# Third of four graph networks: where its last bias is added, how its last product is taken from the banks, and in which batches it is normalized

## The chip, the core and the metric

The kernel runs on one core of one Trainium2 chip. The metric is the device time of one execution in microseconds, as the median of several. The core has five engines with instruction streams of their own: TensorE (PE: matmuls and transposes, with weight loads shown as PEld), VectorE (DVE), ScalarE (ACT), GpSimd (POOL) and SyncE (SP, which here only issues DMAs). They synchronize through semaphores.

## The reference

1250 nodes with 768 features each, 20,000 edges. Four graph networks follow each other, and after each one the result is added to its input and normalized over the features. The third is this (its edge weights are normalized by the degrees, and every node also has an edge to itself):

```python
def _gcn(x, W, b, row, col, ew):
    x = x @ W
    deg = jax.ops.segment_sum(ew, col, num_segments=n) + 1.0
    dinv = jax.lax.rsqrt(deg)
    norm = dinv[row] * ew * dinv[col]
    agg = jax.ops.segment_sum(norm[:, None] * x[row], col, num_segments=n)
    return agg + (dinv * dinv)[:, None] * x + b
h = jax.nn.relu(x @ Wd + bd) @ Wu + bu + x          # 768 -> 24 -> 768
h = jax.nn.relu(_gcn(h, W1, b1, row, col, edge_weight))   # 768 -> 256
h = _gcn(h, W2, b2, row, col, edge_weight)                # 256 -> 768
x = _layernorm(x + h)                                # (v - mean) / sqrt(var + eps)
```

The fourth network starts with two products of every head with 64x64 matrices and then attends along the edges.

## The kernel before

The nodes are cut into NT = 10 tiles of P = 125 rows; `node_b` holds all tiles of the residual (125 x 10 x 768, f32), `node_a` is a buffer of the same size. Each engine has a program of its own. Between phases stands a barrier: `next_phase` (L478 to L482) drains the engine, adds to `phase_end` and waits until all five have done so.

**The phase of the graph sums.** SyncE issues seven loads behind the barrier (L1152 to L1156), the last of them `wadj`, 6250 KB of dense adjacency. TensorE transposes `node_b`, makes the bottleneck product (L1938, L1945), transposes again and makes the product with W1 (L1954). Then it sums over the graph with the dense adjacency, split into a high and a low part: two halves (c = 0 for the first layer, c = 1 for the second), in each ten tiles d, in each tile ten pieces t of three matmuls (L1968). Four banks are in turn, so tile q waits for the take of tile q - 4; the first tile of a half waits, piece by piece, for the low parts of the features (`feature_low`). VectorE takes each sum (`with_own`, two adds), applies the degrees, in the first half also the bias b1 and the relu (L2468, L2469), and makes the low part of the features of the tile before (`row_low_part(1, d - 1, agg1)`, L2447). Behind the first half's loop it makes the low part of tile 9, then the ten tiles of the second half follow.

**The last phase of the third network.** Behind the barrier SyncE issues the weights `gw2` (L1158, 768 KB), the last bias spread over 125 partitions (`gb2_row`, L1159, 375 KB), and eight small loads for the fourth network. TensorE transposes the aggregate (20 transposes), which ScalarE copies out, waits for ten loads on `bulk_loaded`, and makes ten tiles of the product with W2. Each tile has two halves of 384 columns in two banks; with four banks, tile n waits until tile n - 2 has been taken (`mm_taken`). One f32 matmul of the code is two instructions in the profile, so a tile is eight. VectorE does this for each tile, and then normalizes all ten:

```python
for g in range(2):
    v = slice(g * HD, (g + 1) * HD)
    chain.mark(dve.tensor_tensor(node_a[:, n, v], bank[...][0:P, 0:HD], gb2_row[:, v], op=ALU.add))      # L2482
chain.wait()
dve.tensor_tensor(node_b[:, n], node_b[:, n], node_a[:, n], op=ALU.add).then_inc(mm_taken, 1)            # L2484
dve.wait_ge(mm_taken, 2 * NT + n + 1)
dve_stats(dve, chain, node_b, n)                                                                       # L536
```

`dve_norm` is `dve_moments` over all tiles (one `bn_aggr` each, L542, and an add of eps for all, L545), the root of all on ScalarE (`act_sqrt`, L562), and `dve_scale`: a reciprocal (L551) and one scaling of 125x768 for each tile (L553). Then comes the next barrier. Behind it SyncE loads the mask of the fourth network (L1170), and TensorE transposes `node_b` (60 transposes) and makes the fourth network's transform (L1999, L2001).

`iota_row` (128 x 1254) holds the numbers 0, 1, 2, ... by which the second network picks its rows; nothing reads it after that network.

A `Chain` counts instructions of one engine on a semaphore: `mark` has an instruction signal it, `wait` waits for all that were marked.

## Time and profile before

| | us |
|---|---|
| runs | 3425.73, 3424.27, 3413.43; median 3424.27 |
| the profiled execution | 3441.28, of which the profile's span is 3439.5 |
| TensorE busy | 3240.6 |
| VectorE busy | 2173.2 |
| ScalarE busy | 1335.0 |
| GpSimd busy | 922.2 |
| mean granted clock of TensorE | 0.957 of full speed |

The profile is one execution, taken by the hardware profiler. Times in it are us from the span's start. The views used below: the *chain of waits* follows the work that ended last back from the end, each step to what released it; the *timeline* lists instructions in order of time, equal ones merged, with the idle time before them and what ended it in brackets; *stretches* give busy us of each engine with its number of instructions in a window, then the granted clock of TensorE (PEclk: 1.00 is 2.4 GHz, 0.50 is 1.2 GHz), the mean share of the 16 DMA engines that was busy, and what they moved. `arena` is the large buffer in which most tensors lie, `bank` a PSUM bank. SPq and DVEq stand for what an engine's queue did, issues and barriers.

### The profile page before, as it was taken

The page shows a single profiled execution, that of the slowest core. Times are in us where ns is not written, and L with a number is a line of the kernel's source. Part 1 is how long each engine was busy: PE and PEld are TensorE (multiplying, and loading weights), DVE is VectorE, ACT ScalarE, POOL GpSimd, SP SyncE. Part 2 cuts the span into 40 slices and gives each one's busy share as a digit, 9 for nine tenths or more (in the row PEclk, how much of TensorE's full clock was granted, in tenths as well). Part 3 has the DMA queues.
Part 4 walks back from the last instruction along what each step waited for, and adds up shares of the span by engine and source line. Part 5 has one row for each costly group of instructions (what it writes and reads, how often), then busy time and mean ns, then how long its engine had stood idle before and what let it go on. Part 6 is the DMA issues. An engine that isn't in the chain of part 4 may idle for free. (4 is left out here: it accounts for less than half of the span.)

```text
span 3439.5 us, 61775 instructions
## 1 busy us (share of the span) xinstructions
PE 3240.6 (94%) x20813; PEld 3025.1 (88%) x20813; DVE 2173.2 (63%) x4034; ACT 1335.0 (39%) x2527; POOL 922.2 (27%) x968
## 2 busy tenths in 40 slices
PE   6998989999998999999999999999989797899998
PEld 6886778888888999999988999999979495799998
DVE  7898456766777520137878401258868454499998
ACT  1344232333323111124446311134555211388885
POOL 1104534444554310014456200034456000000000
PEclk9999999999999999999999999999999797699997
DMA  3134353423213343347867533367767203000001
GB/s 81 46 105 139 97 137 83 101 50 100 61 31 92 109 142 100 102 157 242 242 207 235 171 111 101 101 203 242 238 204 228 92 1 76 12 1 0 0 0 46
DMA packets 164966, 386.06 MB, mean 112 GB/s; under 512 B 34418, under 2 KB 103583, under 8 KB 164758
## 3 DMA queue, kind: packets, MB, share of 16 engines
q0 software_dynamic: 47200, 173.39, 16.9%
q1 hardware_dynamic: 80074, 147.20, 15.2%
q10 hardware_dynamic: 37484, 62.75, 6.0%
q8 instruction: 124, 2.03, 0.2%
q14 instruction: 84, 0.69, 0.1%
HBM read 283.93 MB, written 99.32 MB: 111 GB/s over the span
## 5 line engine op out<-in xcount | busy, mean ns | idle before, releaser
L1877 PE MATMUL bank<-w_hi,xT_hi 128*125 128x384 f32 x1920 | 650.4, 339 | 0.0
L1878 PE MATMUL bank<-w_lo,xT_hi 128*125 128x384 f32 x1920 | 648.6, 338 | 0.0
L1879 PE MATMUL bank<-w_hi,xT_lo 128*125 128x384 f32 x1920 | 648.5, 338 | 0.0
L1563 ACT COPY arena<-bank 125x384 f32<-125x384 f32 x320 | 153.7, 480 | 793.2 <-PE bank L1879 762.5
L830 POOL DMA_INDIRECT arena<-y_early,edges x204 | 229.4, 1125 | 821.5 <-DMA y_late<-arena 320.4
L904 DVE SCALAR_TENSOR_TENSOR row_lo<-arena,edges,row_hi 128x768 fp32r<-128x768 f32 x300 | 304.2, 1014 | 124.4 <-ACT row_hi L873 84.1
L2345 DVE CAST w_hi<-w_raw 128x2304 fp32r<-128x2304 f32 x35 | 47.6, 1360 | 517.8 <-PE bank L1879 512.5
L1878 PEld LDWEIGHTS bank<-w_lo,xT_hi 128*125 128x125 f32 x1920 | 356.5, 186 | 0.1
L1877 PEld LDWEIGHTS bank<-w_hi,xT_hi 128*125 128x125 f32 x1920 | 356.5, 186 | 0.0
L1879 PEld LDWEIGHTS bank<-w_hi,xT_lo 128*125 128x125 f32 x1920 | 356.3, 186 | 0.1
L743 ACT ACTIVATE arena<-arena,low 125x1250 f32<-125x1250 f32 x170 | 227.7, 1339 | 327.7 <-DVE low L755 327.7
L780 PE MATMUL bank<-arena 125*125 (+1 forms) x2400 | 284.8, 276 | 0.0
L780 PEld LDWEIGHTS bank<-arena 125*125 125x125 f32 x2400 | 281.3, 195 | 0.0
L669 PE MATMUL bank<-h_hi,tsc 125*125 125x512 f32 x800 | 267.4, 408 | 1.3 <-DVE tsc L645 1.3
L1319 POOL DMA_INDIRECT order_d<-row_slot,place_slot x162 | 180.9, 1117 | 321.3 <-DMA order_d<-row_slot,place_slot 265.4
L755 DVE CUSTOM_DVE_ANT_0 arena<-arena 125x1250 f32<-125x1250 f32 x170 | 247.0, 1453 | 9.6 <-DVE arena L749 9.6
L763 PE MATMUL bank<-ident,arena 125*125 125x125 f32 x1700 | 225.9, 281 | 24.6 <-ACT arena L743 11.8
L763 PEld LDWEIGHTS bank<-ident,arena 125*125 125x125 f32 x1700 | 209.3, 195 | 27.7 <-ACT arena L743 17.9
L830 POOL DMA_INDIRECT arena<-y_late,idx_slot x168 | 193.9, 1154 | 126.2 <-issue 55.7
L1299 POOL DMA_INDIRECT w_slot<-inv_d,idx_slot x162 | 177.3, 1094 | 54.3 <-issue 51.5
L873 ACT ACTIVATE row_hi<-arena,edges 128x768 fp32r<-128x768 f32 x204 | 182.0, 932 | 24.6 <-PE bank L963 23.1
L669 PEld LDWEIGHTS bank<-h_hi,tsc 125*125 125x125 f32 x800 | 153.2, 192 | 39.6 <-DVE tsc L645 1.1
(359 smaller groups left out, 6685.7 us busy)
## 6 DMA issues: line engine op xcount, KB each, us to landing
y_early<-arena SPq DMA_DIRECT2D x200, 180.0 KB
w_raw<-in_L_gnn_W_dram ACTq DMA_DIRECT2D x30, 1152.0 KB, 6.4
arena<-own_mask_d SPq DMA_DIRECT2D x50, 585.9 KB
y_late<-arena SPq DMA_DIRECT2D x120, 180.0 KB
h_d<-arena ACTq DMA_DIRECT2D x40, 250.0 KB
arena<-in_L_gnn_W_dram SPq DMA_DIRECT2D x5, 1536.0 KB, 10.8
arena<-h_d ACTq DMA_DIRECT2D x30, 250.0 KB
wadj_d<-arena SPq DMA_DIRECT2D x10, 625.0 KB
```

What stands on the lines that cost most here:

```text
L669: ins = pe.matmul(bank[b][0:P, 0:w], x[:, u % 2, t], y, start=(t == 0 and i == 0), stop=(t == NT - 1 and i == 2))
L743: act.activation(sc, sc, ACT.Exp, scale=-1.0, bias=low[:, d % 4:d % 4 + 1], accum_out=den[:, d % 4:d % 4 + 1]).then_inc(weight_made, 1)
L755: dve.tensor_tensor_reduce(out=sc, in0=sc, in1=mask_row, scale=1.0, scalar=CEILING, op0=ALU.add, op1=ALU.min, accum_out=low[:, d % 4:d % 4 ...
L763: ins = pe.transpose(bank[c][0:P, t * P:(t + 1) * P], sc[:, (t0 + t) * P:(t0 + t + 1) * P], ident[0:P, 0:P])
L780: ins = pe.matmul(bank[b][0:P, 0:w], tsc[:, t], f, start=(t == 0), stop=(t == NT - 1))
L830: pool.indirect_dma_start(gathered[:, k], None, y, bass.IndirectOffsetOnAxis(ap=idx, axis=0)).then_inc(row_landed[k], 16)
L873: act.activation(hi_slot[k % HR], gathered[:, k], ACT.Copy, scale=order[:, p, W_AT:W_AT + 1]).then_inc(high_ready, 1)
L904: dve.scalar_tensor_tensor(lo, gathered[:, k], w, hi.bitcast(F32), op0=ALU.mult, op1=ALU.subtract).then_inc(tile_ready, 1)
L1319: pool.indirect_dma_start(order_d, bass.IndirectOffsetOnAxis(ap=place_slot[:, k:k + 1], axis=0), row_slot[:, k], None).then_inc(order_plac ...
L1877: pe.matmul(b, xT_hi[:, k, v], w_hi[:, h, k], start=(k == 0), stop=False)
L1878: pe.matmul(b, xT_hi[:, k, v], w_lo[:, h, k], start=False, stop=False)
L1879: ins = pe.matmul(b, xT_lo[:, k, v], w_hi[:, h, k], start=False, stop=(k == KD - 1))
```

## The change

The last bias of the third network, `gb2_row`, lies in `iota_row` instead of beside the weights, and is loaded one phase earlier, behind `wadj`, with a semaphore `gb2_loaded` of its own. VectorE adds it to the residual tiles during the first half of the graph sums: tile d behind the low part of tile d - 1, for d from 1 to 9, and tile 0 behind the low part of tile 9. The last product's banks are added straight to `node_b`, and the release of the banks is signalled by the second of these adds. The normalization is split: the moments of tiles 0 to 5 (`HEAD` = 6) come behind the statistics of tile 7, their scalings behind the statistics of tile 8, and the moments and scalings of the other four tiles at the end; ScalarE takes two roots in place of one. The waits on `bulk_loaded` go from ten loads to nine, and VectorE's is replaced by one on its own chain.

```diff
--- before.py
+++ after.py
@@ -381,7 +381,8 @@
         assert gcn_at <= w_at
         gw2 = cut(rest, KG2, D)
         zT = cut(rest + KG2 * D, KG2, N)
-        gb2_row = cut(rest + KG2 * D + KG2 * N, D, parts=P)
+        gb2_row = iota_row[0:P, 0:D]
+        HEAD = NT - 4
         wadj = cut(w_at, NT, NT, CT, parts=P)
         agg1 = cut(gcn_at, NT, G2, parts=P)
         assert gcn_at + NT * G2 <= w_at
@@ -428,6 +429,7 @@
         diag_made, s_spread, s_row_ready = sem("diag_made"), sem("s_spread"), sem("s_row_ready")
         w3_cleared, w3_loaded, w3_turned, w3T_ready = sem("w3_cleared"), sem("w3_loaded"), sem("w3_turned"), sem("w3T_ready")
         iota_ready, bias_loaded = sem("iota_ready"), sem("bias_loaded")
+        gb2_loaded = sem("gb2_loaded")
         far_marked, ln_taken, own_shifted, own_ready = sem("far_marked"), sem("ln_taken"), sem("own_shifted"), sem("own_ready")
         acc_cleared, ln_shifted, own_counted, ln_out = sem("acc_cleared"), sem("ln_shifted"), sem("own_counted"), sem("ln_out")
         mask_stored, mask_loaded = [sem(f"mask_stored{i}") for i in range(2)], sem("mask_loaded")
@@ -1154,9 +1156,9 @@
                          (gw1, a["L2_gnn_W1"].rearrange("(k p) c -> p k c", p=128)), (gb1_row, spread(a["L2_gnn_b1"], P))):
                 sp.dma_start(v, t).then_inc(bulk_loaded, 16)
             sp.dma_start(wadj.rearrange("p d s c -> p d (s c)"), wadj_d.rearrange("d p c -> p d c")).then_inc(wadj_loaded, 16)
+            sp.dma_start(gb2_row, spread(a["L2_gnn_b2"], P)).then_inc(gb2_loaded, 16)
             next_phase(sp)
             sp.dma_start(gw2, a["L2_gnn_W2"].rearrange("(k p) c -> p k c", p=128)).then_inc(bulk_loaded, 16)
-            sp.dma_start(gb2_row, spread(a["L2_gnn_b2"], P)).then_inc(bulk_loaded, 16)
             sp.wait_ge(w3_cleared, 2)
             for i, v in enumerate((a["L3_gnn_attn_l"], a["L3_gnn_attn_r"])):
                 for q in range(2):
@@ -1628,7 +1630,8 @@
                 act.copy(own_hi[1][:, d], agg1[:, d]).then_inc(feature_high, 1)
             next_phase(act)
             act_turn(act, "turn_act", zT, KG2)
-            act_sqrt(act, "sqrt_act", rstd[:])
+            act_sqrt(act, "sqrt_act", rstd[:, 0:HEAD])
+            act_sqrt(act, "sqrt_act", rstd[:, HEAD:NT])
             next_phase(act)
             act_turn(act, "turn_act", xT, KD)
             act.wait_ge(w3_turned, 1)
@@ -1970,7 +1973,7 @@
             next_phase(pe)
             pe_turn(pe, "turn_pe", agg2, KG2)
             pe.wait_ge(piece_taken, counts["turn_pe"])
-            pe.wait_ge(bulk_loaded, 16 * 10)
+            pe.wait_ge(bulk_loaded, 16 * 9)
             for n in range(NT):
                 if n >= 2:
                     pe.wait_ge(mm_taken, 2 * NT + n - 1)
@@ -2469,22 +2472,34 @@
                 dve.tensor_scalar(agg1[:, d], agg1[:, d], 0.0, dinv[:, d:d + 1], op0=ALU.max, op1=ALU.mult).then_inc(sum_taken, 1)
                 if d:
                     row_low_part(1, d - 1, agg1)
+                if d == 1:
+                    dve.wait_ge(gb2_loaded, 16)
+                if d:
+                    chain.mark(dve.tensor_tensor(node_b[:, d], node_b[:, d], gb2_row, op=ALU.add))
             row_low_part(1, NT - 1, agg1)
+            chain.mark(dve.tensor_tensor(node_b[:, 0], node_b[:, 0], gb2_row, op=ALU.add))
             for d in range(NT):
                 with_own(agg2[:, d], 1, d)
                 dve.tensor_scalar(agg2[:, d], agg2[:, d], dinv[:, d:d + 1], None, op0=ALU.mult).then_inc(sum_taken, 1)
             next_phase(dve)
-            dve.wait_ge(bulk_loaded, 16 * 10)
+            chain.wait()
             for n in range(NT):
                 dve.wait_ge(mm_made, 2 * NT + n + 1)
                 for g in range(2):
                     v = slice(g * HD, (g + 1) * HD)
-                    chain.mark(dve.tensor_tensor(node_a[:, n, v], bank[2 * (n % 2) + g][0:P, 0:HD], gb2_row[:, v], op=ALU.add))
+                    ins = dve.tensor_tensor(node_b[:, n, v], bank[2 * (n % 2) + g][0:P, 0:HD], node_b[:, n, v], op=ALU.add)
+                    if g == 0:
+                        chain.mark(ins)
+                ins.then_inc(mm_taken, 1)
                 chain.wait()
-                dve.tensor_tensor(node_b[:, n], node_b[:, n], node_a[:, n], op=ALU.add).then_inc(mm_taken, 1)
                 dve.wait_ge(mm_taken, 2 * NT + n + 1)
                 dve_stats(dve, chain, node_b, n)
-            dve_norm(dve, chain, node_b, node_b)
+                if n == HEAD + 1:
+                    dve_moments(dve, chain, range(HEAD))
+                if n == HEAD + 2:
+                    dve_scale(dve, chain, node_b, node_b, range(HEAD))
+            dve_moments(dve, chain, range(HEAD, NT))
+            dve_scale(dve, chain, node_b, node_b, range(HEAD, NT))
             next_phase(dve)
             for n in range(NT):
                 for g in range(3):
```

## Rows read from the trace of the kernel before

**Rows 1.** The page, busy time of the engines: us, share of the span, instructions.

```profile
PE 3240.6 (94%) x20813; PEld 3025.1 (88%) x20813; DVE 2173.2 (63%) x4034; ACT 1335.0 (39%) x2527; POOL 922.2 (27%) x968
```

**Rows 2.** The chain of waits, third network's last phase: start us, us, what ran.

```profile
2844.80 8.11 DMA arena<-in_L_gnn_b_dram
...
2853.05 4.80 PE bank L1979 x8
...
2857.97 1.03 DVE arena L2482 x2
...
2859.03 0.97 DVE arena L2484
2860.03 1.02 DVE stats L536 x2
...
2887.78 0.87 DVE moments L542 x10
```

**Rows 3.** The timeline of that phase: start us, us, engine, line, operation, count.

```profile
2844.39 2.35 PE L516 MATMUL bank<-ident,arena 125*128 125x125 f32 x20 [1.41 <-DVEq L481]
...
2889.37 5.99 DVE L553 TENSOR_SCALAR arena<-arena,moments,rstd 125x768 f32<-125x768 f32 x10
...
2895.44 1.95 SPq L1170 DMA_DIRECT2D arena<-mask_d  x2
```

**Rows 4.** Stretches of 1 us: busy us by engine, PEclk, DMA share, GB/s.

```profile
2845.00:2846.00 1.00, 1.00 (x12) 1.00 (x11) 0.00 (x0) 0.87 (x2) 0.00 (x0) 1.00 0.49 77
2846.00:2847.00 1.00, 0.75 (x7) 0.51 (x5) 0.00 (x0) 1.00 (x4) 0.00 (x0) 1.00 0.79 224
2847.00:2848.00 1.00, 0.00 (x0) 0.00 (x0) 0.00 (x0) 0.69 (x2) 0.00 (x0) 1.00 1.04 369
2848.00:2849.00 1.00, 0.00 (x0) 0.00 (x0) 0.00 (x0) 0.00 (x0) 0.00 (x0) 1.00 0.81 171
...
2850.00:2851.00 1.00, 0.00 (x0) 0.00 (x0) 0.00 (x0) 0.00 (x0) 0.00 (x0) 0.60 0.51 127
...
2857.00:2858.00 1.00, 1.00 (x5) 0.58 (x4) 0.03 (x1) 0.00 (x0) 0.00 (x0) 0.98 0.00 0
```

**Rows 5.** Who waited for whom; the bottleneck product in the chain, its clock.

```profile
PEld bank L1979 <- DVE arena L2484: 5.3, 8, 0.7
...
2712.76 20.21 PE bank L1945 x32
...
2720.00:2722.00 2.00, 2.00 (x5) 0.94 (x3) 1.77 (x3) 0.00 (x0) 0.00 (x0) 0.50 0.33 136
```

**Rows 6.** Graph sums: TensorE in the chain; VectorE's timeline where the halves meet.

```profile
2772.02 70.97 PE bank L1968 x600
...
2807.46 0.42 DVE L2463 TENSOR_TENSOR arena<-bank,own_hi 125x256 f32<-125x256 f32 x1 [1.43 <-PE bank L1968]
...
2809.17 0.98 DVE L2447 TENSOR_TENSOR own_lo<-arena,own_hi 125x256 fp32r<-125x256 f32 x2
...
2811.03 0.42 DVE L2463 TENSOR_TENSOR arena<-bank,own_hi 125x256 f32<-125x256 f32 x1 [0.88 <-PE bank L1968]
```

**Rows 7.** VectorE's timeline, normalization of the network before in seven and three tiles.

```profile
2671.52 4.22 DVE L553 TENSOR_SCALAR arena<-arena,moments,rstd 125x768 f32<-125x768 f32 x7
...
2677.75 0.35 DVE L542 BATCH_NORM_AGGREGATE moments<-stats 125x2 f32<-125x12 f32 x3
```

**Rows 8.** A stretch of 2 us after the adjacency load, and its first use.

```profile
2740.00:2742.00 2.00, 2.00 (x16) 2.00 (x15) 0.00 (x0) 1.41 (x4) 0.00 (x0) 0.75 0.00 0
...
2745.49 5.99 ACT L1620 CAST adj_hi<-arena 125x1280 fp32r<-125x1280 f32 x5
```

**Rows 9.** Stretches where the clock fell, and the fourth network's transform.

```profile
2690.00:2692.00 2.00, 0.09 (x1) 0.00 (x0) 0.00 (x0) 1.25 (x4) 0.00 (x0) 1.00 0.26 101
2692.00:2694.00 2.00, 1.95 (x4) 0.50 (x5) 0.00 (x0) 0.00 (x0) 0.00 (x0) 0.80 0.31 131
...
2909.00:2976.00 67.00, 67.00 (x213) 57.29 (x212) 11.11 (x27) 9.68 (x26) 0.00 (x0) 0.50 0.30 57
```

## The prediction

> **What bounds the kernel now.** I read the page first, then the chain of waits, then the stretch of the third network engine by engine. The page says that TensorE is busy for 94% of a span of 3439.5 us [rows 1], so a change on VectorE can only pay where TensorE waits. Apart from one load and ten adds in the phase before it, this change acts in the third network's last phase, between the barrier at 2844.4 and the next one at 2895.44, which is 51 us or 1.5% of the span. The chain of waits of that phase [rows 2] has three parts. First comes a DMA: the load of the bias row, issued at 2844.80, ends 8.1 us later, and the product starts at 2853.05, although its transposes were over at 2846.7 [rows 3]. Then comes the first tile, 4.8 us long and mostly at the lower clock. From there to the end the chain is VectorE alone: two adds from the banks (1.03), the add to the residual (0.97), two statistics (1.02), ten times, then the moments, the root and ten scalings of 5.99 us together [rows 2, 3]. VectorE needs 2.97 us for a tile (from the first take at 2857.97, ten tiles end at 2887.7, where the moments begin); TensorE waits for the residual add, up to 0.7 us in each of eight tiles [rows 5]. The last 7.7 us, from 2887.74 to the barrier at 2895.44, have no TensorE work beside them.
>
> **Part 1, the bias load leaves the phase.** It moves to SyncE's queue behind the adjacency load of the phase before, on a semaphore of its own. That earlier load has ended by 2740, since no DMA runs in 2740 to 2742, and the adjacency is first used at 2745.49 [rows 8]. 375 KB behind it, at the 101 to 131 GB/s at which this queue moved shortly before [rows 9], are 3 to 4 us: it lands by 2744, and VectorE wants it only in the graph sums, which begin at 2772 [rows 6], so the load and the new wait cost nothing; if the cover were gone, ScalarE's copies at 2745.49 would be late by at most those 4 us. What remains in front of the product is the weight load, 768 KB. The stretch moved 0.08, 0.22, 0.37 and 0.17 MB in the four microseconds from 2845 to 2849, 0.84 MB together [rows 4], so the weights, issued first, are in at about 2849.0. I let the product start at 2849.2 instead of 2853.05: 3.85 us. Bounds: nothing, if the small loads issued behind (they move up by one place and 0.4 us) hold the weights back as long; 6.3 us, if the product could start when its transposes end. A page of the Trainium skill would put this differently: "DMA: Bandwidth & Descriptors", section on the anatomy of one DMA, gives a fixed cost of about 2.0 us plus bytes over 436 GB/s, by which, as an estimate, the weights land 3.8 us after issue, at 2848.2, and the gain would be 0.8 us more. The rows show 0.70 MB moved by then, less than the weights alone, so I keep the rows.
>
> **Part 2, the clock at the start.** In before, TensorE idled from 2846.7 to 2853.05; its clock fell at 2850.2 and rose again at 2857.0 [rows 4]. The first take came 4.92 us after the product's start [rows 2]; the 3.95 us of it at the lower level cost half of themselves, 2.0, so at the upper level it would be 2.9. Now the idle is about 2.5 us. Whether the clock falls in it is open: after about 2 us of idle in 2690 to 2692 it did fall, within 2692 to 2694 [rows 9]. So I charge half of those 2.0 us; the bounds are 0 and 2. The Trainium skill, "TensorE: Matmul & The Clock Gate", section on why this matters for kernels, asks only that long idle gaps between bursts be avoided, and would call this gap harmless, 1 us better than I say; rows 9 speak against leaning on it. The first take then falls at 2849.2 + 2.9 + 1.0 = 2853.1, 4.9 us earlier than the 2857.97 of before.
>
> **Part 3, the product's tiles.** VectorE's tile loses the residual add: 2.97 - 1.00 = 1.97 us (two adds from the banks, now straight onto the residual in the same shape, and two statistics). The banks come free after 1.0 us instead of 2.0, so TensorE no longer waits and sets the pace: a tile is eight passes over 384 columns, and such a pass takes 20.21/32 = 0.63 us in the bottleneck product, which ran at the lower level [rows 5], so 0.32 at the upper, 2.56 us a tile. With F the first take, tile 7 is taken at F+17.9 and done at F+19.9. Six moments then go in: 0.35 for three and 0.87 for ten [rows 7, 2] give 0.57 for six, 0.8 with the waits: F+20.7, just behind the making of tile 8 at F+20.5. Tile 8 is done at F+22.7. Then come the reciprocal and six scalings, 4.22/7 = 0.6 each [rows 7], 3.9 together: F+26.6. Tile 9, made at F+23.0, waits for that and is done at F+28.6. Its tail is the old one of 7.70 less the moments (0.87 to 0.43) and the scalings (5.99 to 2.45) of six tiles: 3.7. **The phase ends at F+32.3, against F+37.5 before** (2895.44 - 2857.97): 5.2 us. Without the batches it would end at F+23.0+2.0+7.7 = F+32.7, so the batching itself is worth only 0.4 us: VectorE has 0.6 us to spare in a tile, and six scalings of 3.6 us don't fit there; TensorE's work is simply over too soon. Bounds for this part: 4 to 6 us.
>
> **Part 4, ten bias adds in the graph sums.** Each is 125x768 from SBUF, as the residual add of 0.97 is. The graph sums are bound by TensorE, which runs 600 matmuls in 70.97 us without a gap, 3.57 us a tile, and VectorE waits 1.43 us in a first-half tile [rows 6]. So one more add fits into each: VectorE's work on a tile grows from 2.14 to 3.1 us, under 3.57, and it still catches up, only later. One place is tight. The low parts of the last two tiles, 0.98 us from 2809.17, are the inputs of TensorE's first tile of the second half, which is taken at 2811.03; its tenth piece, 0.36 long, begins some 0.65 before that, at 2810.4. The last low part is ready at 2810.15 and now has the add of tile 9 in front of it: ready at about 2810.9, a stall of 0.5 us. Bounds 0 and 1.0, one whole add. The tenth add, of tile 0, stands behind the last low part, where VectorE was idle for 0.88 us before 2811.03, and later tiles have less work still. Costed at nothing: the dropped wait of VectorE, the wait on the chain, given long before, the second root on ScalarE, which is idle otherwise (the first is answered while tile 8 is worked on).
>
> **The sum.** 4.9 (parts 1 and 2) + 5.2 (part 3) - 0.5 (part 4) = 9.6 us, with bounds of 4 and 14 from the parts. From the profiled execution, 3441.28 (the span and 1.8 around it), this gives 3431.7. The median of the three runs shown is 3424.27, 17 us less than that execution, and the prediction is made against it: **3414.7 us**, a ratio of 0.9972. About 0.5%, 17 us, is what a measurement of this kernel can tell from no change, and the three runs alone lie 12 us apart; so I expect "within 0.5%", on the fast side.
>
> **Rivals.** *(A) The clock of the next phase, up.* The fourth network's transform runs from 2909 to 2976 at the lower level for the whole 67 us, though TensorE is busy throughout [rows 9]. It is entered after 10.7 us or more without products (the last take at 2857.97 + 9 x 2.97 = 2884.7, the barrier at 2895.44); that will be 9.3 us now. If the clock stays up there, up to 33 us go: 3382 to 3405. For it: being busy is evidently not all that sets the level, so its entry may matter. Against: the change touches nothing in that phase, and the idle ahead stays longer than those after which the clock fell [rows 4, 9]. 0.10. *(B) The same place, down; this is the slower case.* The profiled execution lies 17 us above the median, which could mean that timed runs of before had part of this stretch at the upper level. If the changed kernel's runs enter it later in that pattern and stay low, they give back 17 to 33 us: 3414.7 + 17 = 3432 up to 3448. It decides once more than 10 us of that stretch change level. 0.07. *(C) The load was not the limit, and the graph sums pay.* The weights land as late as before because the small strided loads move up with them, or VectorE's catching up makes TensorE wait at each early tile. The first takes 3.9 us off the gain, the second at most 9.7 (ten adds of 0.97): 3418.6 to 3424.4. The first is backed by the bias load being only the last of several transfers in flight; 1.43 us of idle per tile speak against the second. 0.17. *That the batches do not do what they say* is in the forecast already, with 0.4 us.
>
> **How the numbers follow.** Forecast 0.66, A 0.10, B 0.07, C 0.17. The likeliest case's own range is 3407 to 3421. For 8 in 10 I go from 3402, into A's upper end, to 3428, which takes in C. Faster by over 0.5% (below 3407) is A and the lower edge of the forecast, where the scatter of the runs adds to the gain: 0.10 + 0.09. Slower by over 0.5% (above 3441) is the upper half of B, 0.03. The rest, 0.78, is within.
>
> **What the changed profile would show.** Right: the product starts 4.5 to 5 us after its barrier instead of 8.7; no wait of TensorE for VectorE in it; 1.97 us of VectorE work per tile; tile 9's take about 3.6 us behind the end of TensorE's last matmul, behind six scalings; about 41 us from barrier to barrier (8.7 of it to the first take, 32.3 behind it) against 51; a gap of half a microsecond on TensorE at the tenth piece of the second half's first tile. Wrong: a product start at 8 us or more, a gap in every graph-sum tile, or a granted clock in the fourth network's transform other than 0.5 in one kernel and 0.5 in the other, which would outweigh everything above.

## The result, and the profile after

The changed kernel's median is **3401.53 us** (12 runs, 3395.44 to 3418.39). The kernel before, run twelve times beside it, has 3412.52 (3406.46 to 3430.15). The ratio is 0.9957, with an interval of [0.9939, 0.9974]: 11.0 us less by the medians, 8.9 to 20.8 us by the interval. That is within 0.5% of no change, as forecast, but 13 us under the time forecast and 0.5 us under the range. The profiled execution took 3402.10 us, of which 3400.4 are the span, at a mean granted clock of 0.966. Two single runs of the kernel before, of 13999.35 and 4565.12 us, are left out of the comparisons below.

First the chain of waits of the changed kernel, from the last tiles of the graph sums' first half to the start of the fourth network (start, us, what; the pieces named "issue" are left out):

```profile
2774.14 35.41 PE bank L1971 x300
...
2811.37 0.33 DVE own_lo L2450
2811.71 0.87 DVE arena L2478
2812.57 0.35 DVE own_lo L2450
2812.97 32.73 PE bank L1971 x273
...
2847.07 4.98 DMA arena<-in_L_gnn_W_dram
2852.19 22.48 PE bank L1982 x64
2874.69 1.03 DVE arena L2490 x2
2875.82 1.03 DVE stats L538 x2
2876.88 0.58 DVE moments L544 x6
...
2879.82 3.62 DVE arena L555 x6
2883.45 0.94 DVE arena L2490 x2
2884.48 1.03 DVE stats L538 x2
2885.53 0.44 DVE moments L544 x4
```

It answers to [rows 2]. The DMA in front of the product is now the weight load and not the bias; behind it comes one piece of TensorE, eight tiles long, where before VectorE's adds, residual add and statistics alternated. VectorE takes over only with the take of tile 7 (2874.69). The timeline of the same phase (start, us, engine, line, operation, tensors, then the idle time before it and what ended it):

```profile
2852.19 27.63 PE L1982 MATMUL bank<-arena 128*125 128x384 f32 x80 [2.74 <-DMA arena<-in_L_gnn_W_dram]
2856.73 1.02 DVE L2490 TENSOR_TENSOR arena<-bank,arena 125x384 f32<-125x384 f32 x2 [9.73 <-PE bank L1982]
...
2859.21 1.02 DVE L2490 TENSOR_TENSOR arena<-bank,arena 125x384 f32<-125x384 f32 x2 [0.34 <-PE bank L1982]
...
2886.65 2.45 DVE L555 TENSOR_SCALAR arena<-arena,moments,rstd 125x768 f32<-125x768 f32 x4
2889.17 2.10 SPq L1172 DMA_DIRECT2D arena<-mask_d  x2
```

The 80 matmuls of the product run without a gap for 27.63 us, and now VectorE is the one that waits, 0.34 us between the first two tiles. Measured from the first issue behind the barrier (2847.07) to the first issue behind the next (2889.17), the phase takes 42.10 us; the same stretch is 51.07 us in the profile of before (2844.37 to 2895.44). So the phase gave 9.0 us. In the phase before it, VectorE's takes of the two tiles where the halves meet are further apart than the usual 3.57:

```profile
2809.58 0.42 DVE L2466 TENSOR_TENSOR arena<-bank,own_hi 125x256 f32<-125x256 f32 x1 [0.57 <-PE bank L1971]
...
2811.62 0.95 DVE L2478 TENSOR_TENSOR arena<-arena,iota_row 125x768 f32<-125x768 f32 x1
2812.49 0.42 DVE L2450 TENSOR_TENSOR own_lo<-arena,own_hi 125x256 fp32r<-125x256 f32 x1
2812.83 0.95 DVE L2480 TENSOR_TENSOR arena<-arena,iota_row 125x768 f32<-125x768 f32 x1
2813.70 0.42 DVE L2466 TENSOR_TENSOR arena<-bank,own_hi 125x256 f32<-125x256 f32 x1
```

Here it is 4.12 us: the bias add of tile 9 (L2478) stands before the last low part (L2450), for which TensorE waits until 2812.97 in the chain. The graph sums give back 0.6 us. The change's work is thus worth **8.4 us in the profiles**.

**What else differs between the two profiled executions.** They lie 39.2 us apart (3441.28 and 3402.10), and the work explains 8.4. The rest is the sum of 34.3 us less in the fourth network's transform, which the change does not touch, and 3.6 us more in other stretches (2.1 ahead of the graph sums' end, 1.5 behind the transform). Two stretches of the profile after (columns: length, busy us of PE, PEld, DVE, ACT and POOL with their instructions, granted clock, DMA share, GB/s):

```profile
2852.00:2854.00 2.00, 1.81 (x3) 1.16 (x4) 0.00 (x0) 0.00 (x0) 0.00 (x0) 0.50 0.12 26
...
2899.00:2939.00 40.00, 39.26 (x240) 35.54 (x240) 12.32 (x29) 11.45 (x32) 0.00 (x0) 1.00 0.58 114
```

The second is the transform, at the upper level from end to end, where [rows 9] had it at the lower one for 67 us. From the barrier to VectorE's last copy of its results (2939.48 here, 2980.07 in the profile of before) it takes 50.3 us here and 84.6 there. A run's mean granted clock goes with its time: 3401 to 3402 us at 0.965 or 0.966, 3395.44 at 0.969, 3418.39 at 0.961. The first row belongs to the product's first tile, below.

### The profile page after: what moved, and what is told of

Same layout as the page of the kernel before. It is cut to its first block and busy times, and to the rows that moved or that the text cites. A ratio compares the mean times of both kernels' runs of the same rounds, so it can differ in the third digit from the quotient of the medians.

```text
span 3400.4 us, 61788 instructions
## 1 busy us (share of the span) xinstructions
PE 3208.0 (94%) x20813; PEld 3003.0 (88%) x20813; DVE 2172.7 (64%) x4036; ACT 1335.6 (39%) x2528; POOL 926.5 (27%) x968
```

## The experiments

Twelve kernels ran on three chips, with the kernel before beside them each time: on the first the changed kernel again, the one with one batch, the load alone and all but the load; on the second the kernel before, the wide gap, the filled gap and "both"; on the third the others. "Phase" below is the stretch measured as above, from the barrier behind the graph sums to the next, in the profile of each (where the weights come a phase earlier, it starts with TensorE's first transpose). Two more figures are needed for the comparison of whole runs. "Low" is the number of runs whose mean granted clock was 0.962 or less. "At equal clock" is a least-squares fit, for the runs of one chip together, of the time on the mean granted clock plus a constant for each kernel; on the first two chips it gives -2.8 us per 0.001 of clock, with 3.4 us of scatter left, and on the third -1.8, with 3.0. The number behind +- is a 95% interval. Such a fit also takes away what a kernel gains by keeping its clock up in the phase itself, so it can come out below the phase's gain.

### The two kernels again

The changed kernel, unedited, and one in which every hunk of the change is taken back again.

> The changed kernel again, more runs. Theory 1 (the local gain is all there is): the phase between its two barriers takes 42 us instead of 51, the graph sums 0.6 us more, so 8.5 to 9 us at equal clock states, and what goes beyond that is the level of the clock in the fourth network's transform (67 us at the lower level cost 34 us more), which differs from run to run in both kernels. Then fast runs with the same mean granted clock differ by 8.5 to 9 us, and the median ratio lies at 0.9970 to 0.9980 unless one side had more low runs. Theory 2 (the change makes the transform run at the upper level more often): the kernel before shows runs with a mean clock near 0.957 or 0.961 clearly more often than this one, and the ratio stays at 0.9957 or below.

The changed kernel has 3404.85 (9 runs) against 3418.18 (31 runs), ratio 0.9943 [0.9913, 0.9974], and at equal clock -8.8 +- 2.7 us. Its phase takes 42.0 us, its transform 50.2, as in the first profile. So the 8.4 us read from the trace are the change's work, as theory 1 has it, and by the fit the rest of the 13 us between these medians goes with the clock: 12 of 31 runs of before were low, and 1 of 9. That the ratio lies below 0.9957 and the low runs are unevenly spread is what theory 2 asks for; more on it below.

> The kernel before in the place of a changed one, for a second profile of it, its runs with their clocks, and as the null of the comparison. In the session before this one, 12 of 31 runs of it lay above 3425 us at mean clocks of 0.952 to 0.962, and no run of four variants did (39 runs). Theory 1 (chance levels of the clock in the fourth network's transform, the same for every kernel): this label shows the ratio 1.000 within its interval, and its low-clock runs are as frequent as those of the variants. Theory 2 (something in the kernel before makes the low level more frequent): a third or more of these runs lie above 3425 us, with mean clocks of 0.962 or less, and runs of the same clock state still differ from the changed kernel's by 8.5 to 9.5 us.

3414.72 (12 runs) against 3412.2 (35 runs), ratio 1.0003 [0.9982, 1.0024]. That profile again has a phase of about 50.7 us, but 64.6 for the transform, of which 27 us were at the lower level, against 68 in the profile of before (the last row is of that one):

```profile
2903.00:2904.00 1.00, 1.00 (x9) 0.89 (x8) 0.00 (x0) 0.31 (x1) 0.00 (x0) 0.95 0.89 175
2904.00:2930.00 26.00, 26.00 (x84) 22.21 (x82) 4.67 (x11) 3.79 (x11) 0.00 (x0) 0.50 0.78 151
2932.00:2955.00 23.00, 22.73 (x139) 20.42 (x139) 7.46 (x18) 6.56 (x18) 0.00 (x0) 1.00 0.00 1
...
2936.00:2976.00 40.00, 40.00 (x127) 34.17 (x128) 6.80 (x16) 5.87 (x16) 0.00 (x0) 0.50 0.00 0
```

In both profiles of before the clock fell 1.7 to 1.8 us behind the transform's first matmul, with TensorE busy: **one and the same program stays at the lower level for 27 us in one execution and for 68 in another**. 5 of 12 runs were low, 9 of 35 beside it, and of the sign of theory 2, a third of these runs above 3425 us, little came: 1 of 12. By themselves the changed kernel's runs are too few to say that it is low less often: 3 of 21 were, against 12 of 31, 9 of 35 and, on the third chip, 1 of 17 of before. All runs together point that way. A clock of 0.960 or less stands beside 15 of 95 runs of before (9 of 31, 6 of 47, 0 of 17 by chip) and beside 2 of 95 of the changed kernel and its relatives below, the wide gap left out (1 of 39, 0 of 22, 1 of 22, and 0 of 12 in the first comparison). The some 7 us at the lower level that the change saves around its own phase are worth 0.001 of mean clock, and with 0.961 as the bound for the relatives it would be 4 of 95. Also, none of the eleven profiles of those kernels has the lower level in the transform, where both profiles of before have it. Why is open: the kernel with the load alone, whose code ahead of the transform is that of before, did not show it either.

### The parts of the change

**One batch.** The scalings of all ten tiles stand behind the last tile again.

```diff
-            act_sqrt(act, "sqrt_act", rstd[:, 0:HEAD])
-            act_sqrt(act, "sqrt_act", rstd[:, HEAD:NT])
+            act_sqrt(act, "sqrt_act", rstd[:])
...
-                if n == HEAD + 1:
-                    dve_moments(dve, chain, range(HEAD))
-                if n == HEAD + 2:
-                    dve_scale(dve, chain, node_b, node_b, range(HEAD))
-            dve_moments(dve, chain, range(HEAD, NT))
-            dve_scale(dve, chain, node_b, node_b, range(HEAD, NT))
+            dve_norm(dve, chain, node_b, node_b)
```

> The changed kernel with one normalization of all ten tiles at the end. Theory 1 (TensorE's work ends too soon for the six scalings to hide): the phase takes 0.4 us longer than in the changed kernel, 42.5 us. Rival (the scalings of six tiles do hide beside the product): 3.5 us longer, 45.5 us.

3407.93 (10 runs), ratio 0.9950 [0.9922, 0.9978]; the phase takes 42.8 us, 0.7 more than with batches. The end of its chain:

```profile
2855.27 27.74 PE bank L1981 x80
2883.04 1.03 DVE arena L2489 x2
2884.17 1.03 DVE stats L538 x2
2885.22 0.87 DVE moments L544 x10
```

TensorE is the chain through all ten tiles here, and 7.7 us of normalization follow as in [rows 2]. With batches TensorE carries eight tiles, and then six scalings of 3.62 us stand between tile 8 and tile 9. Taken out of the tail, they go in front of the last tile, where VectorE has only its 0.4 us of idle per tile for them. The batching is worth 0.7 us, near the 0.4 of the prediction, and not the 4.0 by which the tail gets shorter (7.7 to 3.7). The whole runs (0.9950, and 0.9943 for the changed kernel) are too coarse to show it.

**The load alone.** The kernel before, in which only the bias load and its semaphore move (the place of the row and the two waits, left out here, as in the change).

```diff
+            sp.dma_start(gb2_row, spread(a["L2_gnn_b2"], P)).then_inc(gb2_loaded, 16)
             next_phase(sp)
             sp.dma_start(gw2, a["L2_gnn_W2"].rearrange("(k p) c -> p k c", p=128)).then_inc(bulk_loaded, 16)
-            sp.dma_start(gb2_row, spread(a["L2_gnn_b2"], P)).then_inc(bulk_loaded, 16)
```

> The kernel before with the bias row loaded one phase earlier and nothing else. Theory 1 (the bias load held the product's start back): the product starts 5.1 us after the barrier instead of 8.7, its first tile is taken 3.9 us earlier, and as VectorE sets the pace from there at 2.97 us a tile, the phase takes 47.2 us instead of 51.1. Rival (the take of the bias through the same banks is what matters, the start is hidden): under 1 us less than 51.1.

3415.28 (10 runs), ratio 0.9972 [0.9946, 0.9997], at equal clock -4.6 +- 2.5 us. The phase takes 48.5 us, 2.6 less than before. The chain shows why it is neither the 3.9 expected nor 3.2:

```profile
2850.30 5.32 DMA arena<-in_L_gnn_W_dram
2855.76 5.47 PE bank L1980 x8
2861.35 1.03 DVE arena L2483 x2
```

The product starts 5.46 us after the barrier instead of 8.68 (3.2 us), but the first tile takes 5.47 us instead of 4.80 [rows 2], since all of it lies at the lower level (until 2861.6), where in before the clock rose at 2857.0, within the tile.

**All but the load.** The changed kernel with a second copy of the bias row loaded where it used to be, and waited for (ten loads again).

```diff
             sp.dma_start(gw2, a["L2_gnn_W2"].rearrange("(k p) c -> p k c", p=128)).then_inc(bulk_loaded, 16)
+            sp.dma_start(cut(rest + KG2 * D + KG2 * N, D, parts=P), spread(a["L2_gnn_b2"], P)).then_inc(bulk_loaded, 16)
```

> The changed kernel, and besides a second copy of the bias row is loaded at the old place into the old place, and TensorE waits for it as before; nothing reads it. Theory 1: the product starts 8.7 us after the barrier again, the first take comes at 13.6, and the phase takes 46.0 us instead of 42.1. Rival (the gain comes from the shorter tiles alone): it stays within 1 us of 42.1.

3412.75 (10 runs), ratio 0.9971 [0.9946, 0.9996], at equal clock -6.9 +- 2.5. The phase takes 45.2 us, and the bias load is the chain's again:

```profile
2845.54 7.67 DMA arena<-in_L_gnn_b_dram
2853.35 22.43 PE bank L1983 x64
```

The load is worth 3.1 us of the phase from this side and 2.6 from the other; the adds and batches are worth 5.9. The two parts alone make 8.5 us, both together 9.0: they hardly touch each other.

**Without the ten adds.** The bias is left out altogether, so the third network's result lacks it; VectorE's wait for the row moves to the product.

```diff
-                if d == 1:
-                    dve.wait_ge(gb2_loaded, 16)
-                if d:
-                    chain.mark(dve.tensor_tensor(node_b[:, d], node_b[:, d], gb2_row, op=ALU.add))
             row_low_part(1, NT - 1, agg1)
-            chain.mark(dve.tensor_tensor(node_b[:, 0], node_b[:, 0], gb2_row, op=ALU.add))
```

> The changed kernel without the ten adds of the bias in the graph sums; the last bias is left out of the result. Theory 1 (the adds cost TensorE one stall of 0.5 to 0.6 us where the halves meet, and nothing else): from the first graph sum to the barrier it takes 72.4 us instead of 72.9, with no wait of TensorE at the low part of tile 9. Rival (they cost more through a busier memory or later takes): over 1 us less.

The graph sums are one piece of the chain, as long as in [rows 6]:

```profile
2778.50 70.97 PE bank L1971 x600
```

So the 0.6 us are due to the adds, by the change's trace to the one add in front of the last low part, and the other nine cost nothing. One run took 3405.61 us, at a clock of 0.965.

### What sets the level in the transform

**A wider gap ahead of it.** ScalarE makes four copies of 125x768 just before it hands TensorE the transposed matrices, so TensorE waits about 3 us more behind its transposes.

```diff
             act.wait_ge(w3_turned, 1)
+            for n in range(4):
+                act.copy(res3[:, n], node_b[:, n])
             act.copy(logit3.rearrange("p k i q -> p (k i q)"), bank[7][:, 0:4 * KD]).then_inc(w3T_ready, 1)
```

> The changed kernel with four copies of 125x768 on ScalarE (into a place that is overwritten later) ahead of the two small copies for which TensorE waits between its transposes and the fourth network's transform: the idle there grows from 1.4 us to 4 us or more. Theory (what TensorE did just ahead of the transform decides its level, since its own work doesn't lift the clock from the lower level): most of its runs go through the transform at the lower level, 3 us of the gap and some 34 us of the clock later than the changed kernel, 3435 us or more, mean clock 0.957. Rival (the level there is not tied to the gap): 3 us later and otherwise the same mix as the changed kernel.

3429.03 (10 runs, 3405.71 to 3440.72), ratio 1.0044 [1.0014, 1.0074]: **8 of 10 runs were low**, against 9 of 35 of before on the same chip and 3 of 21 of the changed kernel. On the same chip the kernel with the filled gap, below, has a median 25.1 us less; by the ratios (1.0044 against 0.9943 and 0.9957) it is 30 to 34 us against the changed kernel. So the 3 us cost far more than 3. The edit also moves the transform's start and has ScalarE copy ahead of it, so that the idle itself is the cause is likely, but not separated from these. The profile caught one of the milder executions (3414.14 us):

```profile
2892.00:2894.00 2.00, 0.00 (x0) 0.00 (x0) 0.00 (x0) 2.00 (x5) 0.00 (x0) 0.55 0.95 188
2894.00:2916.00 22.00, 21.83 (x69) 18.69 (x70) 3.39 (x8) 3.10 (x9) 0.00 (x0) 0.50 0.87 173
2916.00:2940.00 24.00, 24.00 (x149) 21.96 (x148) 7.65 (x18) 6.71 (x18) 0.00 (x0) 1.00 0.03 4
```

The clock falls in the idle, and stays at 0.50 (1.2 GHz) for 22 us of matmuls with TensorE busy for 99% of them, before it rises in the middle of the same loop. At the end of these 22 us the DMA share drops too, from 0.87 to 0.03; but the transform of the profile after ran at the upper level with a share of 0.58, and that of before stayed at the lower one for 40 us with a share of 0.00 (2936 to 2976, above), so the transfers are not the cause.

**The gap filled.** Two matmuls more, into a free bank, where TensorE waits for ScalarE's last copies.

```diff
+            pe.wait_ge(piece_taken, counts["turn_pe"] - 3)
+            for _ in range(2):
+                pe.matmul(bank[(counts["turn_pe"] - 4) % 6][:, 0:HD], ident[:], xT[:, 0, 0:HD], start=True, stop=True)
             pe.wait_ge(w3T_ready, 2)
```

> The changed kernel with two matmuls of 128x384 (four instructions, a product nobody reads) between TensorE's transposes and the transform, in the place of 1.3 of the 1.4 us of idle. Theory: no run goes through the transform at the lower level, so the few high runs of the changed kernel (3413 to 3423 us, clock 0.960 to 0.962) are gone and the spread is below 10 us; the median is the changed kernel's, within 2 us. Rival (the level is not tied to the gap): the same high runs in about one of six.

3403.93 (10 runs), ratio 0.9977 [0.9960, 0.9995], at equal clock -6.4 +- 2.4 (its phase and graph sums give 9.7). None of the 10 runs was low, which can't be told apart from 3 of 21; and the runs still spread over 17 us (3394.4 to 3411.74), where less than 10 was expected. Other stretches lie at the lower level as well: in each of the fourteen profiles between 48 and 65 us behind the transform, and 27 us around the bottleneck product. So the wide gap brings the low level on, while the filled one does not visibly do more than the changed kernel already does.

### What is left in the phase

**The weights a phase earlier.** They go into a free part of the buffer, issued once the product with W1 is over (at 2778.48, where the graph sums begin).

```diff
-        gw2 = cut(rest, KG2, D)
+        gw2 = cut(xT_at + 2 * NT * G2, KG2, D)
...
-            next_phase(sp)
+            sp.wait_ge(mm_made, 2 * NT)
             sp.dma_start(gw2, a["L2_gnn_W2"].rearrange("(k p) c -> p k c", p=128)).then_inc(bulk_loaded, 16)
+            next_phase(sp)
```

> The changed kernel with the last product's weights loaded one phase earlier, nothing else. Theory 1 (the start is set by the load, then by the transposes' copies): the product starts 3.4 us after the barrier instead of 5.1, the clock stays up, the first take comes 6.4 us after the barrier instead of 9.7, and the phase takes 38.8 us instead of 42.1. Rival (the clock falls all the same): 40.4 us.

3407.34 (10 runs), ratio 0.9968 [0.9957, 0.9980]; the phase takes 38.8 us, 3.3 less than the changed kernel's. The chain in front of the product is ScalarE's copies now:

```profile
2851.28 0.66 PE bank L519 x4
2852.02 2.56 ACT arena L527 x6
2854.63 20.92 PE bank L1984 x64
```

TensorE is idle for only 0.99 us ahead of the product and keeps its clock: eight tiles take 20.92 us instead of 22.48. The phase is the 38.8 us expected. The whole runs don't show the step: the ratio of 0.9968 is no lower than the changed kernel's 0.9957 and 0.9943, on other chips.

**The scalings on ScalarE.** Batches of five, three and two; ScalarE scales the first eight tiles with a bias of minus mean times root.

```diff
+                for d in range(t0, t1):
+                    act.activation(node_b[:, d], node_b[:, d], ACT.Identity, bias=minus_mean[:, d:d + 1], scale=rstd[:, d:d + 1]).then_inc(ln_done, 1)
```

> The changed kernel with the scalings of eight tiles on ScalarE, the weights loaded where they were. Theory 1 (the six scalings on VectorE hold up tile 9's take, and four more stand at the end): the phase ends 27.6 us behind the first take instead of 32.4, 37.3 us between the barriers instead of 42.1. Rival (ScalarE's 0.94 us a tile and the roots queued behind them hold up the end): over 39 us.

3403.02 (5 runs), ratio 0.9962 [0.9940, 0.9983]. The phase takes 39.0 us, less gain than expected: the clock had fallen ahead of the product and stayed down longer than in the changed kernel (granted 0.53 in 2862 to 2864, 10 us behind the weight load's issue, where the changed kernel was up after 8.3), so the first take came 10.85 us after that issue instead of 9.66. That is 1.2 us; behind the first take the phase is 4.3 us shorter (28.2 instead of 32.4; 27.6 expected). So the phase lies at the edge of the rival's "over 39", but for 1.2 of the 1.7 us through the clock and not through ScalarE.

**Both.** The weights a phase earlier, and the scalings on ScalarE, in one kernel.

> A version meant to beat the changed kernel. The scalings of tiles 0 to 4 and 5 to 7 go to ScalarE (idle there), VectorE gives it the reciprocal and the negated scaled mean and scales tiles 8 and 9 itself; and the last product's weights are loaded one phase earlier, behind TensorE's last read of the old transposed features, into a free part of their place. Theory, from the changed kernel's profile (42.1 us between the barriers, first take 9.7 us after the first, 32.4 to the second): the product starts 3.4 us after the barrier instead of 5.1 and at the upper level, so the first take comes at 6.4, and VectorE has only 2.0 of 2.56 us in a tile, so the phase ends 27.5 us behind it: 34 us, 8 us less than the changed kernel, a ratio of about 0.995 to the kernel before at equal clocks, 17 us. Rival (the activation function changes ScalarE's table at each root): two to four table loads of 1 to 2 us, and the phase takes 36 to 38 us.

3392.70 (12 runs, 3388.02 to 3401.23), ratio **0.9940 [0.9917, 0.9962]**, with no low run, and a phase of 34.15 us, as expected. Its median is 11.2 us under that of the changed kernel with the filled gap on the same chip. At equal clock it is -11.1 +- 2.4 against before, less than the expected 17; the fit takes away the clock that the phase keeps, and whether that is all of the difference is open. The timeline of ScalarE and of the first take:

```profile
2845.48 26.07 PE L1990 MATMUL bank<-arena 128*125 128x384 f32 x80 [0.99 <-ACT arena L529]
2848.46 1.02 DVE L2498 TENSOR_TENSOR arena<-bank,arena 125x384 f32<-125x384 f32 x2 [6.43 <-PE bank L1990]
...
2866.51 4.70 ACT L1641 ACTIVATE arena<-arena,minus_mean,rstd 125x768 f32<-125x768 f32 x5 [2.12 <-DVE minus_mean L2511]
...
2871.74 2.86 ACT L1641 ACTIVATE arena<-arena,minus_mean,rstd 125x768 f32<-125x768 f32 x3 [0.44 <-DVE minus_mean L2511]
```

ScalarE scales a tile in 0.94 us, slower than VectorE's 0.6, but beside VectorE's own work, so the batching pays at last: it does when the batch goes to an engine that has room. Between root and scalings ScalarE's timeline shows a wait for VectorE (0.44 us in front of the second batch) and no table load, so the rival's loads did not occur. The phase is 17 us shorter than before (51.07 to 34.15).

**Both, with TensorE kept busy.** Six idle matmuls before the barrier and the two of the filled gap are added.

> The faster version (scalings on ScalarE, weights early) with matmuls that nobody reads in two idle places of TensorE: six of 128x384 behind the last product, during the last tile's normalization (3.8 of 4.8 us), and two between the transposes and the fourth network's transform (1.3 of 1.4 us). Theory: the clock stays up over the barrier, so the 60 transposes take 7 us instead of 8.5, and the transform never runs at the lower level: 1.5 us less than the version without them, and no run with a clock of 0.965 or less. Rival (keeping the clock up here spends it elsewhere, since the version without them already goes through the transform at the upper level): the transposes get faster, but the median stays within 2 us of that version's.

3397.13 (6 runs) against 3419.41 (17 runs), ratio 0.9941 [0.9925, 0.9956]. In its profile the clock is 1.00 throughout the phase (the first row) and the transform (the second):

```profile
2847.00:2883.00 36.00, 33.64 (x125) 20.70 (x126) 24.10 (x61) 11.13 (x19) 0.36 (x2) 1.00 0.05 5
2883.00:2931.00 48.00, 46.45 (x298) 41.68 (x296) 13.16 (x32) 18.39 (x49) 0.00 (x0) 1.00 0.65 129
```

From the barrier to the end of the transform it takes 48.8 us where the kernel above takes 50.5. The ratio doesn't show these 1.7 us. These two kernels beat the changed one as well as before; the filler is not shown to add anything.

## Why the prediction was right and wrong

**The start of the product: the load right, 0.3 us short.** The weights' own load became the limit and not the small loads behind it. It starts the product 5.12 us after the barrier, not 4.83; rival C's first form (the weights as late as before) did not occur. The moved load cost its own phase nothing that shows: from that phase's first issue to the first graph sum it takes 89.3 us in the changed kernel's profile and 91.3 in that of before.

**The clock at the start: the step that failed in the phase.** The steps charged half of 2.0 us. The rows above have the clock at 0.50 right behind the 2.74 us of idle, and it rises only in 2855 to 2856. The first take came 4.54 us after the product's start instead of 3.9, and 9.66 after the barrier instead of 8.7. Half was a mean of two outcomes neither of which is half. With the clock kept, the first take comes 2.95 to 2.98 us after the product's start (the kernels with a wide or filled gap and with the early weights), as the prediction's 2.9 for the upper level had it; with the clock lost, 4.35 to 5.6 us (4.54 in the changed kernel's profile, 5.6 in the kernel with the load alone and the one with ScalarE's scalings). The phases of the kernels that have the changed kernel's code in it fall apart likewise, 40.6 and 40.75 us (wide and filled gap) against 42.0 to 42.1, with the same load in front; the wide gap's profile has the upper level where the changed kernel's has 0.50:

```profile
2845.00:2847.00 2.00, 1.55 (x5) 1.04 (x6) 0.00 (x0) 0.00 (x0) 0.00 (x0) 1.00 0.14 29
```

The Trainium skill, "TensorE: Matmul & The Clock Gate", section on why this matters for kernels, warns of long idle gaps alone and would have charged nothing here. Of the eight profiles with the weight load alone in front of the product, six lost the clock and two kept it, so the rule holds for a quarter of them.

**The tiles: right.** TensorE set the pace, no wait of TensorE for VectorE appears in the product, and from the first take to the next barrier it took 32.44 us (32.3 predicted, 37.5 before). The batching was worth 0.7 us (0.4 predicted).

**The ten adds: right.** One stall of 0.6 us where the halves meet (0.5 predicted), nothing elsewhere. Rival C's second form, nine or more adds paid for, did not occur.

**The sum.** 3.94 + 5.03 - 0.59 = 8.4 us against 9.6 predicted. The difference is the start of the product (0.3), the clock (0.6), the tiles (0.2) and the adds (0.1).

**The time: wrong by the anchor.** The step that failed is the sentence that sets the sum against the median of the three runs shown. They were 3425.73, 3424.27 and 3413.43, and two of them lie in the upper part of what this kernel does: of twelve runs only one is above 3425.73, and their median is 3412.52. 3412.52 - 9.6 would have been 3402.9, within 1.4 us of the result. That the medians lie 11.0 us apart, near the 9.6 of the sum, is in part luck: 8.4 of them are read from the traces as the change's work. That the profiled execution lay 17 us above the median, and the three runs 12 us apart, was in the text, and both pointed at a scatter which three runs don't pin down; the range's low edge of 3402 lay only 5 us under the lower edge of 3407 that the likeliest case had of itself, where the twelve runs of before span 24 us.

**Rivals A and B: their mechanism is real, and varies from run to run.** The transform at the upper level gives 34.3 us (84.6 to 50.3), as A had it, and it appears between the two profiled executions: the sign that the prediction named as outweighing everything, a level other than 0.5 in one of the two, did come. But the same program shows 84.6 and 64.6 us, so comparing single profiles would have credited the change with more than four times its worth. That what happens ahead of the transform matters is shown by the kernel with the wide gap. A's argument against itself, that the change touches nothing there, is not safe: over all runs the low level is rarer in the kernels that carry the change or its load (2 of 95 against 15 of 95); for the changed kernel alone it is not shown, and the cause is open. It could account for the part of the 11.0 us between the medians that exceeds 8.4; the clocks of the runs of before in that comparison are not on record.

## What to carry over

Before a sum is set against a median, look at how far the runs scatter and at their granted clocks: where single runs scatter by more than the expected gain, the median of three of them is not a fixed point, and the range has to hold its error besides the sum's. A clock that may or may not fall is two cases with a price each, not half a price. And moving work out of a tail pays only as far as the engine that gets it has idle time earlier: six scalings on VectorE gave 0.7 us, eight given to ScalarE gave 4.3 more.

## What the runs showed of the hardware

- TensorE can be busy for 99% of 22 us at 0.50 of its clock and then go on at 1.00 in the same loop, without a change in what it runs; in the two profiles of before this lasted 68 and 27 us, and began 1.7 to 1.8 us into the loop, behind 1.2 us of idle. The run time follows: about -2.8 us for 0.001 of mean granted clock on two chips, -1.8 on the third.
- 3 us more of idle ahead of that loop, with ScalarE's copies in it, went with 8 of 10 low runs, at a cost of 25 us by the medians of one chip.
- After 2.7 to 3.1 us of idle ahead of the product the clock was lost in six profiles and kept in two (idle of 2.8 and 3.0 us); after 1.0 us it was kept in three of three.
- A load of 768 KB landed 4.98 to 5.32 us after its issue in the eight profiles where nothing went with it but small loads. The Trainium skill, "DMA: Bandwidth & Descriptors", section on the anatomy of one DMA, would make this 3.8 us as an estimate (2.0 us plus bytes over 436 GB/s), but it gives that fit for DMAs issued from GpSimd, and this one is issued from SyncE; the measured landing decides.
- The issue of the 375 KB bias load behind the 6250 KB one occupied SyncE for 39.6 us in the changed kernel's profile, where the issues before it took 0.3 to 0.7 us each. It had nothing else to issue in that phase, so nothing waited.
- ScalarE's scaling of 125x768 f32 with a bias and a scale for each partition took 0.94 us, and VectorE's 0.60.
